# One hardware loop for the middle head groups, and the sum of |weight| gathered in one step instead of three

## The chip, the cores and the metric

The kernel runs on one core of a Trainium2 chip. The metric is the device time of one execution in microseconds (us); the kernel before took 2062.81 us, the median of three executions.

## The reference

Causal attention over 16 heads, then a feed-forward layer with ternary weights and 8-bit activations, and a residual:

```python
q, k, v = proj(x, Wq), proj(x, Wk), proj(x, Wv)      # x: 8 x 512 x 1024, fp32
scores = (q * beta) @ k.T / 8, causal; attn = softmax(scores)
a = (attn @ v) @ Wo.T
alpha = max(mean(|weight|), 1e-5)                     # one number
q_w = clip(round(weight / alpha), -1, 1) * alpha
q_a = round(a / s) * s,  s = max|a| over the row / 127
out = x + q_a @ q_w.T + bias
```

The scale alpha needs the sum of |weight| over the whole 1024 x 1024 matrix before the first weight can be rounded.

## The kernel before

The work is an order written out by hand, one list per engine. There are 4 groups `g` of 4 heads and 8 batches; a pair (group, batch) is an iteration `it`, 32 in all. Each iteration projects q, k and v for its batch (TensorE, `J(gi, k)`, line 170, in 8 accumulation groups `gi`), and has 16 units `u` = 4 heads x 4 query tiles. One unit is: scores `S(u)` (TensorE, lines 253 and 254), mask and row minimum `M(u)` (VectorE, 265), exponential `E(u)` (ScalarE, 272), reciprocal `I(u)` (VectorE, 278), normalisation (GpSimd, 284), transpose `T(u)` (TensorE, 294), its high part `H(u)` (ScalarE, 308) and low part `L(u)` (VectorE, 315). `PV(h)` (TensorE, 330) multiplies a head by v, `OL(h)` (ScalarE, 339) and `OA(h)` (VectorE, 347) add up its two halves. `V(gi)` takes a projection out of PSUM: the high part on ScalarE (201, 211, 217), the low part on VectorE (224, 231, 235). Every fp32 operand is split so into two parts.

A step overlaps the projections of iteration `now` with the later units of iteration `old` and the loading of x for `nxt`. `program` (line 682) calls the step function of each engine 33 times. The six inner batches of groups 0, 1 and 2 are hardware loops over `b`; the two steps between groups, which also split new weights (`qk_for`, `v_for`), and all steps of the last group are written out, so that their semaphore counts are constants.

The six inner steps of the last group carry `wf_part` = 0 to 5 and prepare the ternary weight. The weight comes as 8 tiles of 512 KB into two buffers (`load_wf`, line 448, on SP's DMA queue), once for the sum and once more for the rounding, 16 loads in all. A load waits until the tile two before it has been used. `wf_abs` (ScalarE, line 460) takes |tile| and its row sums:

```python
elif n < KT + 2:
    if due(count := n - 1):
        sp.wait_ge(wf_abs_done, count)
...
act.wait_ge(wf_in[k % 2], (k // 2 + 1) * 16)
act.activation(wf_raw[k % 2], wf_raw[k % 2], ACT.Abs, accum_out=wf_sums[:, k:k + 1])\
```

`wf_add_partitions` (TensorE) and `wf_scale` (VectorE) make alpha; `wf_ternary` (VectorE, three operations a tile) rounds. The sums of tiles 0 and 1 are taken late in the step of part 0, tiles 2 to 5 in part 1, tiles 6 and 7 early in part 2; alpha falls in part 2, and the rounding is in parts 2 to 5, two tiles each. SP issues the loads of the first two tiles right behind the four loads of x for the next iteration (`load_x`), and those of later tiles after the store of an output block (`store_o`) or around the two copies of k (`swap_k`).

After the last step, the output projection and the feed-forward layer run over 32 tiles of tokens.

Of the kernel before, what the change touches and what calls it, by code (L numbers as in the profile page):

```python
# [14 lines left out]
KT = D // P  # L15
HG = 4
NG = D // DH // HG
# [19 lines left out]
def adaln_ffn_kernel(nc, x, xT, cond, wq, wk, wv, wo, wf, bias, out):  # L37

    oT = nc.dram_tensor("oT_scratch", (KT, P, B, S), F32, kind="Internal").ap()
    with ExitStack() as ctx:  # L40
# [419 lines left out]
        def wf_abs(act, k):  # L460
            act.wait_ge(wf_in[k % 2], (k // 2 + 1) * 16)
            act.activation(wf_raw[k % 2], wf_raw[k % 2], ACT.Abs, accum_out=wf_sums[:, k:k + 1])\
               .then_inc(wf_abs_done, 1)
# [218 lines left out]
        def program(eng, step):  # L682
            step(eng, None, (0, 0, 0), (1, 1))
            with eng.Fori(1, B - 1) as b:
                step(eng, (b - 1, 0, b - 1), (b, 0, b), (b + 1, b + 1))
            for g in range(1, NG - 1):
                it = g * B
                step(eng, (it - 2, g - 1, B - 2), (it - 1, g - 1, B - 1), (it, 0), qk_for=g)
                step(eng, (it - 1, g - 1, B - 1), (it, g, 0), (it + 1, 1), v_for=g)
                with eng.Fori(1, B - 1) as b:  # L690
                    it = g * B + b
                    step(eng, (it - 1, g, b - 1), (it, g, b), (it + 1, b + 1))

            it, g = STEPS - B, NG - 1
            step(eng, (it - 2, g - 1, B - 2), (it - 1, g - 1, B - 1), (it, 0), qk_for=g)
            step(eng, (it - 1, g - 1, B - 1), (it, g, 0), (it + 1, 1), v_for=g)
            for b in range(1, B - 1):
                it = g * B + b
                step(eng, (it - 1, g, b - 1), (it, g, b), (it + 1, b + 1), wf_part=b - 1)
            it = STEPS - 1  # L700
            step(eng, (it - 1, g, B - 2), (it, g, B - 1), None, last=True)
            step(eng, (it, g, B - 1), None, None, last=True)

        def pe_step(pe, old, now, nxt, qk_for=None, v_for=None, wf_part=None, last=False):
            o, n, g = old and old[0], now and now[0], now and now[1]

            def J(gi, *ks):
                if now:
                    for k in ks:
                        project(pe, n, g, gi, k)  # L710

            def S(u):
                if u >= 8 and old:
                    scores(pe, o, u)
                elif u < 8 and now:
                    scores(pe, n, u)

            def T(u):
                if u >= 6 and old:
                    transpose(pe, o, u)  # L720
                elif u < 6 and now:
                    transpose(pe, n, u)

            def PV(h):
                if old:
                    times_v(pe, o, h)

            def Y(t, half, *ks):
                if last and not now:
                    for k in ks:  # L730
                        attention_out(pe, t, t, half, k)

            J(0, 0, 1, 2)
            S(8)
            T(6)
            J(0, 3, 4)
            PV(0)
            J(0, 5)
            S(9)
            T(7)  # L740
            J(0, 6, 7)
            J(1, 0)
            Y(0, 0, 0)
            S(10)
            T(8)
            J(1, 1, 2, 3)
            Y(0, 0, 1, 2, 3)
            S(11)
            T(9)
            J(1, 4)  # L750
            PV(1)
            J(1, 5, 6)
            Y(0, 0, 4, 5)
            S(12)
            T(10)
            J(1, 7)
            J(2, 0, 1)
            Y(0, 0, 6, 7)
            S(13)
            Y(0, 1, 0)  # L760
            T(11)
            J(2, 2, 3, 4)
            Y(0, 1, 1, 2)
            S(14)
            T(12)
            PV(2)
            J(2, 5, 6, 7)
            Y(0, 1, 3, 4)
            S(15)
            Y(0, 1, 5)  # L770
            T(13)
            J(3, 0, 1, 2)
            Y(0, 1, 6, 7)
            if wf_part == 2:
                wf_add_partitions(pe, n)
            S(0)
            T(14)
            J(3, 3, 4, 5)
            Y(1, 0, 0, 1)
            S(1)  # L780
            T(15)
            J(3, 6, 7)
            J(4, 0)
            Y(1, 0, 2, 3, 4, 5)
            S(2)
            T(0)
            PV(3)
            J(4, 1, 2, 3, 4, 5, 6)
            Y(1, 0, 6, 7)
            S(3)  # L790
            T(1)
            J(4, 7)
            J(5, 0, 1, 2, 3, 4)
            S(4)
            T(2)
            J(5, 5, 6, 7)
            J(6, 0, 1, 2)
            S(5)
            T(3)
            J(6, 3, 4, 5, 6, 7)  # L800
            J(7, 0)
            S(6)
            T(4)
            J(7, 1, 2, 3, 4, 5, 6)
            S(7)
            T(5)
            J(7, 7)

        def act_step(act, old, now, nxt, qk_for=None, v_for=None, wf_part=None, last=False):
# [3 lines left out]
            def E(u):  # L813
                if u >= 7 and old:
                    exponent(act, o, u)
                elif u < 7 and now:
                    exponent(act, n, u)

            def H(u):
                if u >= 5 and old:  # L820
                    pt_high(act, o, u)
                elif u < 5 and now:
                    pt_high(act, n, u)
# [15 lines left out]
                if qk_for is not None:  # L839
                    split_w_qk(act, n, qk_for, gi, False)  # L840

            def F(part, k):
                if wf_part == part:
                    wf_abs(act, k)

            if not old:
                split_w_qk(act, -1, 0, 0, False)
# [18 lines left out]
                split_w_v(act, o, v_for, False)  # L866
            H(6)
            E(8)
            F(1, 2)
            F(2, 6)  # L870
            OL(0)
            H(7)
            E(9)
            F(1, 3)
            F(2, 7)
            V(0)
            H(8)
            if ending:
# [2 lines left out]
            if ending:  # L881
                wo_high(act, 7)
                o_high(act, 1, 1)
            H(9)
            E(11)
            OL(1)
            H(10)
            E(12)
            V(1)
            H(11)  # L890
            E(13)
            H(12)
            E(14)
            F(0, 0)
            F(1, 4)
            OL(2)
            H(13)
            V(2)
            E(15)
            F(0, 1)  # L900
            F(1, 5)
            W(0)
            H(14)
            E(0)
# [32 lines left out]
        def dve_step(dve, old, now, nxt, qk_for=None, v_for=None, wf_part=None, last=False):  # L937
# [36 lines left out]
                    split_w_qk(dve, n, qk_for, gi, True)  # L974

            def Q(half):
                if wf_part is not None and 2 <= wf_part < 2 + KT // 2:
                    wf_ternary(dve, 2 * (wf_part - 2) + half)

            if not old:  # L980
                batch_scale(dve, 0, 0)
# [49 lines left out]
            L(13)  # L1031
            V(2)
            I(15)
            if wf_part == 2:
                wf_scale(dve, n)
            M(0)
            Q(0)
# [73 lines left out]
        def sp_step(sp, old, now, nxt, qk_for=None, v_for=None, wf_part=None, last=False):  # L1111
            ending = last and not now
            if not old:
                load_w(sp, 0, [0])
                load_x(sp, 0, 0)
                load_w(sp, 0, [1, 2])
            if qk_for is not None:
                load_w(sp, qk_for, [0, 1, 2])
            if nxt:
                load_x(sp, *nxt)  # L1120
            if wf_part == 0:
                load_wf(sp, 0)
                load_wf(sp, 1)
            if last and now:
                load_o(sp, 0, 0)
                load_o(sp, 1, 1)
            if ending:
                load_wo(sp, 6)
                load_wo(sp, 7)
            if old:  # L1130
                store_o(sp, *old, 0)
            if ending:
                load_o(sp, 2, 0)
            if wf_part == 1:
                load_wf(sp, 4)
                load_wf(sp, 5)
            if wf_part == 2:
                load_wf(sp, KT)
                load_wf(sp, KT + 1)
            if now:  # L1140
                swap_k(sp, now[0], 0)
            if last and now:
                load_wo(sp, 0)
                load_wo(sp, 1)
            if now:
                swap_k(sp, now[0], 1)
            if wf_part is not None and 2 <= wf_part < 1 + KT // 2:
                load_wf(sp, KT + 2 * wf_part - 2)
            if last and now:
                load_wo(sp, 2)  # L1150
            if old:
                store_o(sp, *old, 1)
            if wf_part is not None and wf_part < 2:
                load_wf(sp, 4 * wf_part + 2)
                load_wf(sp, 4 * wf_part + 3)
            if wf_part is not None and 2 <= wf_part < 1 + KT // 2:
                load_wf(sp, KT + 2 * wf_part - 1)
            if last and now:
                load_wo(sp, 3)
                load_wo(sp, 4)  # L1160
                load_wo(sp, 5)
# [133 lines left out]
```

## Time and profile before

| | us |
|---|---|
| median of three executions (2062.33 to 2063.89) | 2062.81 |
| the profiled execution's own time | 2063.89 |
| its span, first to last instruction | 2062.1 |
| TensorE busy, share of the span | 99% |
| VectorE, ScalarE, GpSimd busy | 62%, 49%, 39% |
| granted TensorE clock, mean | 0.999 |
| HBM read and written | 126.36 MB, 33.55 MB |

Times of the trace count from the start of the span. A busy share is an average: it tells what an engine did over the whole span, not whether it was waited for at a given place.

### The profile page before, as it was taken

Reading aid. Unit: us, or ns where it says so; the run is one execution under the profiler, and the core shown is the slowest. Engines: PE = TensorE matmul, PEld = TensorE weight load, DVE = VectorE, ACT = ScalarE, POOL = GpSimd, SP = SyncE. Lnnn points to the kernel's source line nnn. Section 1 sums busy time; section 2 is a strip of 40 time slices with the busy share of each in tenths; the row PEclk is TensorE's granted clock in tenths of the full one; section 3 lists DMA queues with packets and bytes.
Section 4 is the critical chain, followed back from the end, with each engine's and each line's share of the span. In section 5 each row is a group of like instructions: output and inputs, shape, how many; then the busy total and the mean of one; then the engine's idle time right before and its main releaser. Section 6 shows DMA issues by size and latency. Waiting matters only on the chain.

```text
span 2062.1 us, 36378 instructions
## 1 busy us (share of the span) xinstructions
PE 2035.6 (99%) x11747; PEld 1725.0 (84%) x11778; DVE 1274.7 (62%) x3163; ACT 1010.7 (49%) x2383; POOL 803.8 (39%) x746
## 2 busy tenths in 40 slices
PE   8999999999999999999999999999999999999998
PEld 7888888888888888888888888888887777777775
DVE  5666666766666667666666766667766545455454
ACT  5656556655656566666565766656565000000000
POOL 3433333433333334344433433333334544444441
PEclk9999999999999999999999999999999999999999
DMA  4222223222222242222224223323223432333322
GB/s 164 72 73 89 92 71 138 77 78 72 71 72 71 79 140 72 72 71 71 72 89 155 73 98 115 121 93 93 92 72 104 137 122 92 112 101 104 109 98 75
DMA packets 85936, 194.51 MB, mean 94 GB/s; under 512 B 7392, under 2 KB 40160, under 8 KB 84320
## 3 DMA queue, kind: packets, MB, share of 16 engines
q1 hardware_dynamic: 85856, 193.50, 29.3%
q8 instruction: 44, 0.72, 0.1%
q14 instruction: 36, 0.29, 0.0%
HBM read 126.36 MB, written 33.55 MB: 78 GB/s over the span
## 4 chain that ended last, share of the span: by engine, by line
PE 48%; issue 30%; POOL 19%; ACT 1%; DVE 1%; POOLq 1%; DMA 0%; DVEq 0%; SPq 0%; ACTq 0%
PE proj_ps L170 18%; POOL prob L284 12%; PE s_ps L563 9%; PE proj_ps L563 8%; POOL parts L374 7%; PE o_ps L634 5%; PE t_ps L294 3%; PE o_ps L330 2%; PE s_ps L254 1%; PE s_ps L253 1%; PE t_ps L612 1%; ACT parts L370 0%; POOLq L283 0%; DMA w_raw<-wq 0%; ACT v_st L201 0%
## 5 line engine op out<-in xcount | busy, mean ns | idle before, releaser
L170 PE MATMUL proj_ps<-parts 128*128 128x512 f32 (+1 forms) x6144 | 1214.3, 345 | 10.1 <-DVE parts L374 10.1
L170 PEld LDWEIGHTS proj_ps<-parts 128*128 128x128 f32 x6144 | 929.9, 190 | 119.5 <-issue 10.1
L284 POOL TENSOR_TENSOR prob<-prob,row_inv 128x128 f32<-128x128 f32 (+3 forms) x512 | 393.4, 771 | 932.3 <-DVE row_inv L278 929.9
L265 DVE CUSTOM_DVE_ANT_0 prob<-s_ps,mask 128x128 f32<-128x128 f32 (+3 forms) x512 | 249.8, 488 | 340.3 <-PE t_ps L294 194.3
L308 ACT ACTIVATE pt_hi<-t_ps 128x128 fp32r<-128x128 f32 (+3 forms) x512 | 222.3, 434 | 434.7 <-PE t_ps L294 430.4
L272 ACT ACTIVATE prob<-prob,row_min 128x128 f32<-128x128 f32 (+3 forms) x512 | 286.3, 559 | 72.9 <-DVE row_min L265 66.9
L315 DVE TENSOR_TENSOR pt_lo<-t_ps,pt_hi 128x128 fp32r<-128x128 f32 (+3 forms) x512 | 249.5, 487 | 65.5 <-ACT pt_hi L308 59.9
L619 ACT ACTIVATE yt_q<-t_ps 128x1024 bf16<-128x1024 bf16 x32 | 32.8, 1025 | 428.0 <-PE t_ps L612 428.0
L294 PE MATMUL t_ps<-ident,prob 128*128 128x128 f32 x1280 | 227.7, 276 | 7.3 <-POOL prob L284 5.7
L374 POOL TENSOR_TENSOR parts<-x_raw,parts 128x512 fp32r<-128x512 f32 x128 | 203.1, 1607 | 51.5 <-ACT parts L370 51.5
L563 PE MATMUL proj_ps<-parts 128*128 128x512 f32 x768 | 186.2, 396 | 0.0
L563 PE MATMUL s_ps<-parts 128*128 128x512 f32 x768 | 185.1, 396 | 0.0
L294 PEld LDWEIGHTS t_ps<-ident,prob 128*128 128x128 f32 x1280 | 150.8, 140 | 32.0 <-POOL prob L284 8.1
L563 PEld LDWEIGHTS s_ps<-parts 128*128 128x128 f32 x768 | 142.9, 188 | 30.6
L563 PEld LDWEIGHTS proj_ps<-parts 128*128 128x128 f32 x768 | 142.6, 188 | 30.3
L254 PE MATMUL s_ps<-k_st,q_st 128*128 128x128 f32 (+3 forms) x512 | 164.9, 322 | 0.0
L330 PE MATMUL o_ps<-pt_lo,v_st 128*128 128x512 f32 (+3 forms) x512 | 157.6, 319 | 0.5 <-DVE v_st L224 0.5
L253 PE MATMUL s_ps<-k_sw,q_st 128*128 128x128 f32 (+3 forms) x512 | 158.0, 309 | 0.0
L370 ACT ACTIVATE parts<-x_raw 128x512 fp32r<-128x512 f32 x256 | 147.0, 622 | 1.7 <-PE proj_ps L170 0.3
L330 PE MATMUL o_ps<-pt_hi,v_st 128*128 128x512 f32 (+3 forms) x512 | 146.5, 323 | 0.0
L374 DVE TENSOR_TENSOR parts<-x_raw,parts 128x512 fp32r<-128x512 f32 x128 | 135.8, 1080 | 8.1 <-ACT parts L370 8.0
L653 POOL TENSOR_TENSOR x_bias<-x_tile,bias_bc 128x1024 f32<-128x1024 f32 x32 | 76.2, 2384 | 105.2 <-DVE res L663 92.9
(65 smaller groups left out, 1902.9 us busy)
## 6 DMA issues: line engine op xcount, KB each, us to landing
x_raw<-xT SPq DMA_DIRECT2D x128, 512.0 KB, 5.5
k_sw<-k_st SPq DMA_DIRECT2D x128, 256.0 KB, 3.7
oT_scratch<-o_sum SPq DMA_DIRECT2D x64, 256.0 KB, 2.3
x_raw<-oT_scratch SPq DMA_DIRECT2D x32, 512.0 KB, 4.6
x_tile<-x SPq DMA_DIRECT2D x32, 512.0 KB, 5.2
out<-res SPq DMA_DIRECT2D x32, 512.0 KB, 3.1
w_raw<-wf SPq DMA_DIRECT2D x16, 512.0 KB, 5.6
w_raw<-wq SPq DMA_DIRECT2D x4, 1024.0 KB, 7.0
```

Of the source, the lines that this page charges most:

```text
L170: mm = pe.matmul(out, l, r, start=(k == 0 and i == 0), stop=(k == KT - 1 and i == 2))
L253: pe.matmul(s_ps[u % 2][:, 0:w], q, k_sw[:, h, 0:w], start=True, stop=False)
L254: pe.matmul(s_ps[u % 2][:, 0:w], q, k_st[:, h, 0:w], start=False, stop=True).then_inc(s_done, 1)
L265: dve.tensor_tensor_reduce(prob[:, u % 4, 0:w], s_ps[u % 2][:, 0:w], mask[:, S - w:S], 1.0, -MASKED, ALU.add, ALU.min, row_min[:, u % 4:u ...
L272: act.activation(prob[:, u % 4, 0:w], prob[:, u % 4, 0:w], ACT.Exp, bias=row_min[:, u % 4:u % 4 + 1], scale=-1.0, accum_out=row_sum[:, u % ...
L284: pool.tensor_tensor(prob[:, u % 4, 0:w], prob[:, u % 4, 0:w], row_inv[:, u % 4:u % 4 + 1].broadcast_to([P, w]), ALU.mult).then_inc(norm_d ...
L294: mm = pe.transpose(t_ps[u % 2][:, kb * P:(kb + 1) * P], prob[:, u % 4, kb * P:(kb + 1) * P], ident[:, :])
L308: act.activation(pt_view(pt_hi[h % 2], qt), t_ps[u % 2][:, 0:(qt + 1) * P] .rearrange("p (k q) -> p k q", q=P), ACT.Copy).then_inc(pt_hi_d ...
L315: dve.tensor_tensor(pt_view(pt_lo[h % 2], qt), t_ps[u % 2][:, 0:(qt + 1) * P] .rearrange("p (k q) -> p k q", q=P), pt_view(pt_hi[h % 2], q ...
L330: mm = pe.matmul(o_ps[h % 2][:, q0:S], v, part[h % 2][:, kb, q0:S], start=(kb == 0 and part is pt_lo), stop=(kb == QT - 1 and part is pt_hi))
L374: eng.tensor_tensor(x_lo[:, k, :], x_raw[:, k, :], x_hi[:, k, :].bitcast(F32), ALU.subtract).then_inc(x_lo_done[k % 2], 1)
L563: mm = pe.matmul(y_ps[p][half][:, :], a[p][:, o], b[k][:, w], start=(k == 0 and i == 0), stop=(k == KT - 1 and i == 2))
```

## The change

Two edits. The steps of groups 1 and 2 go into one hardware loop over `g` around the loop over `b`, so that the iteration number is made of two registers. And the eight sums of |tile| all go into the step of part 0, spread over ScalarE's list from behind `E(8)` on; alpha is made in part 1 and the rounding is in parts 1 to 4. SP's loads move with them.

```diff
-            for g in range(1, NG - 1):
+            with eng.Fori(1, NG - 1) as g:
                 it = g * B
...
-            if wf_part == 2:
+            if wf_part == 1:
                 wf_add_partitions(pe, n)
...
-            def F(part, k):
-                if wf_part == part:
-                    wf_abs(act, k)
+            def F(*ks):
+                if wf_part == 0:
+                    for k in ks:
+                        wf_abs(act, k)
...
             H(6)
             E(8)
-            F(1, 2)
-            F(2, 6)
+            F(0)
             OL(0)
             H(7)
             E(9)
-            F(1, 3)
-            F(2, 7)
+            F(1)
             V(0)
             H(8)
...
+            F(2)
             H(9)
             E(11)
+            F(3)
             OL(1)
             H(10)
+            F(4)
             E(12)
             V(1)
+            F(5)
             H(11)
             E(13)
+            F(6)
             H(12)
             E(14)
-            F(0, 0)
-            F(1, 4)
             OL(2)
+            F(7)
             H(13)
             V(2)
             E(15)
-            F(0, 1)
-            F(1, 5)
...
-                if wf_part is not None and 2 <= wf_part < 2 + KT // 2:
-                    wf_ternary(dve, 2 * (wf_part - 2) + half)
+                if wf_part is not None and 1 <= wf_part <= KT // 2:
+                    wf_ternary(dve, 2 * (wf_part - 1) + half)
...
             if nxt:
                 load_x(sp, *nxt)
             if wf_part == 0:
-                load_wf(sp, 0)
-                load_wf(sp, 1)
+                for i in range(6):
+                    load_wf(sp, i)
...
                 store_o(sp, *old, 0)
...
-            if wf_part == 1:
-                load_wf(sp, 4)
-                load_wf(sp, 5)
-            if wf_part == 2:
-                load_wf(sp, KT)
-                load_wf(sp, KT + 1)
+            if wf_part == 0:
+                load_wf(sp, 6)
             if now:
                 swap_k(sp, now[0], 0)
+            if wf_part == 0:
+                for i in range(7, KT + 2):
+                    load_wf(sp, i)
```

In parts 1 to 3 SP then loads the tiles 2 to 7 for the rounding at the same two places, before and after `store_o` of block 1, where parts 2 to 4 had them.

## Rows read from the trace of the kernel before

**Rows 1.** The page: busy time, share and instructions of each engine.

```profile
PE 2035.6 (99%) x11747; PEld 1725.0 (84%) x11778; DVE 1274.7 (62%) x3163; ACT 1010.7 (49%) x2383; POOL 803.8 (39%) x746
```

**Rows 2.** Timeline of PE, first product of `PV(0)` in six steps: start, duration, instruction.

```profile
443.73 0.39 PE L330 MATMUL o_ps<-pt_lo,v_st 128*128 128x512 f32 x1
...
687.33 0.39 PE L330 MATMUL o_ps<-pt_lo,v_st 128*128 128x512 f32 x1
...
736.06 0.39 PE L330 MATMUL o_ps<-pt_lo,v_st 128*128 128x512 f32 x1
...
1223.00 0.39 PE L330 MATMUL o_ps<-pt_lo,v_st 128*128 128x512 f32 x1
...
1320.29 0.39 PE L330 MATMUL o_ps<-pt_lo,v_st 128*128 128x512 f32 x1
...
1515.63 0.39 PE L330 MATMUL o_ps<-pt_lo,v_st 128*128 128x512 f32 x1
```

**Rows 3.** Timeline of SP in the step of part 0: start, time to issue.

```profile
1224.47 1.77 SPq L362 DMA_DIRECT2D x_raw<-xT  x4
1226.29 1.13 SPq L458 DMA_DIRECT2D w_raw<-wf  x2
...
1238.13 0.47 SPq L241 DMA_DIRECT2D k_sw<-k_st  x1
```

**Rows 4.** Issue to landing of single loads of wf, issued at 1226.29.

```profile
DMA to landing us min/median/max: 8.4/8.4/8.4
```

**Rows 5.** The same for loads issued at 1353.02, 1401.68 and 1407.67.

```profile
DMA to landing us min/median/max: 5.6/5.6/5.6
...
DMA to landing us min/median/max: 5.2/5.2/5.2
...
DMA to landing us min/median/max: 3.6/3.6/3.6
```

**Rows 6.** Timeline of ACT in the step of part 0, with idle time before.

```profile
1223.28 0.19 ACT L272 ACTIVATION_READ_ACCUMULATOR prob<-prob,row_min 128x1 f32 x1
...
1226.14 0.60 ACT L308 ACTIVATE pt_hi<-t_ps 128x512 fp32r<-128x512 f32 x1 [1.13 <-PE t_ps L294]
...
1227.54 1.40 ACT L211 ACTIVATE q_st<-proj_ps,q_scale 64x512 fp32r<-64x512 f32 x2 [0.31 <-PE proj_ps L170]
...
1232.13 0.72 ACT L272 ACTIVATE prob<-prob,row_min 128x512 f32<-128x512 f32 x1 [0.32 <-DVE row_min L265]
...
1236.09 1.20 ACT L217 ACTIVATE k_st<-proj_ps 64x512 fp32r<-64x512 f32 x2
...
1241.89 1.04 ACT L462 ACTIVATE w_raw<-w_raw 128x1024 f32<-128x1024 f32 x1
...
1243.05 0.60 ACT L339 ACTIVATE o_low<-o_ps 64x512 f32<-64x512 f32 x1
...
1244.93 1.38 ACT L211 ACTIVATE q_st<-proj_ps,q_scale 64x512 fp32r<-64x512 f32 x2
```

**Rows 7.** Timelines of POOL and DVE there: normalisation of units 9 and 15, `M(11)`.

```profile
1227.61 0.62 POOL L284 TENSOR_TENSOR prob<-prob,row_inv 128x256 f32<-128x256 f32 x1 [1.86 <-DVE row_inv L278]
...
1247.49 1.04 POOL L284 TENSOR_TENSOR prob<-prob,row_inv 128x512 f32<-128x512 f32 x1 [4.40 <-DVE row_inv L278]
...
1231.40 0.69 DVE L265 CUSTOM_DVE_ANT_0 prob<-s_ps,mask 128x512 f32<-128x512 f32 x1
```

**Rows 8.** Timeline of PE there: the transposes `T(9)` and `T(15)`.

```profile
1231.01 0.38 PE L294 MATMUL t_ps<-ident,prob 128*128 128x128 f32 x2
...
1249.36 0.60 PE L294 MATMUL t_ps<-ident,prob 128*128 128x128 f32 x4
```

**Rows 9.** Stretches: length, busy and count of each engine, granted clock, DMA share, GB/s.

```profile
10.10:14.80 4.70, 4.69 (x11) 3.69 (x12) 4.52 (x3) 3.12 (x7) 4.70 (x4) 1.00 1.03 432
20.00:24.70 4.70, 4.70 (x22) 3.68 (x21) 3.79 (x4) 1.83 (x3) 0.00 (x0) 1.00 0.70 279
...
2052.60:2056.00 3.40, 3.40 (x10) 1.23 (x9) 0.00 (x0) 0.00 (x0) 0.00 (x0) 0.50 0.38 154
```

More of the change, by code:

```diff
@@ L1033, in dve_step @@
             I(15)
-            if wf_part == 2:
+            if wf_part == 1:
                 wf_scale(dve, n)
@@ L1133, in sp_step @@
                 load_o(sp, 2, 0)
-            if wf_part == 1:
-                load_wf(sp, 4)
-                load_wf(sp, 5)
-            if wf_part == 2:
-                load_wf(sp, KT)
-                load_wf(sp, KT + 1)
+            if wf_part == 0:
+                load_wf(sp, 6)
             if now:
                 swap_k(sp, now[0], 0)
+            if wf_part == 0:
+                for i in range(7, KT + 2):
+                    load_wf(sp, i)
             if last and now:
@@ L1146, in sp_step @@
                 swap_k(sp, now[0], 1)
-            if wf_part is not None and 2 <= wf_part < 1 + KT // 2:
-                load_wf(sp, KT + 2 * wf_part - 2)
+            if wf_part is not None and 1 <= wf_part < KT // 2:
+                load_wf(sp, KT + 2 * wf_part)
             if last and now:
@@ L1152, in sp_step @@
                 store_o(sp, *old, 1)
[L1153 to L1157, printed above, removed]
+            if wf_part is not None and 1 <= wf_part < KT // 2:
+                load_wf(sp, KT + 2 * wf_part + 1)
             if last and now:
```

## The prediction

> **What bounds the kernel now.** I read the page first: TensorE is busy 99% of the span [rows 1]. So an edit can win little, and whatever makes TensorE wait is lost in full, since no later stage has idle time in which to make it good. Then I read the timeline of TensorE at the same mark of each step, the first product of `PV(0)`, to see what a step costs in its two forms [rows 2]. From 443.73 to 687.33 lie five steps of a hardware loop, each with a jump back: 48.72 us a step. From 687.33 to 736.06 lies the last one, which leaves the loop: 48.73. The two written-out steps from 1223.00 to 1320.29 (part 0 and part 1, with six of the eight sums) take 48.65 each, and the four from 1320.29 to 1515.63 (alpha and the rounding) 48.84 each. Last I read SP's, ScalarE's and the other engines' timelines within the step of part 0 and the landing of the loads, because the second edit puts all its work there.
>
> **The first edit, one loop over g.** Four steps that were written out (two between groups, for g = 1 and 2) get register counts. The loop form costs 48.72 - 48.65 = 0.07 us a step [rows 2], so 4 x 0.07 = 0.28 us. The twelve inner steps have one register more in their counts. No row shows such a step. Below, this costs nothing (counts may be kept in one register); above, as much again as the step from constants to one register did, 12 x 0.07 = 0.84. I take 0.2, nearer the lower end, since TensorE mostly has matmuls in its queue while its sequencer works; both ends stay for the range. The outer jump back is taken once. The inner jumps cost nothing that can be seen: 48.72 with them, 48.73 without [rows 2]. So I put it at nothing; its cover is the work already queued, and without that it would be well under a microsecond.
>
> [...]
>
> **The second edit, what only moves.** The eight sums are the same instructions. So are alpha and the 24 operations of the rounding; they come one step earlier, beside the same neighbours, and four steps keep their 48.84 - 48.65 = 0.19 us each. That is nothing net. The cover is the idle time of ScalarE and VectorE in steps that TensorE fills.
>
> **The second edit, the first tile.** Here lies the cost. Before, the first sum stands behind `E(14)`, at 1241.89 [rows 6]. Now `F(0)` stands right behind `E(8)`, whose last part starts at 1223.28 and ends at 1223.47 [rows 6]. But its tile is not there. SP issues the load behind the four loads of x, at 1226.29 [rows 3], and those four wait for the splits of x in this very step; neither is moved. The load takes 8.4 us to land, because 2 MB of x are ahead of it [rows 4]: 1234.7. ScalarE works in order. It stands at `F(0)` from 1223.5 to 1234.7, and behind it stand `OL(0)`, `H(7)`, `E(9)`, `V(0)` and all the rest; for `E(9)` waits `I(9)`, then the normalisation on GpSimd, then `T(9)`, and TensorE works in order too.
>
> The time at which `T(9)` can go follows in steps. A sum takes 1.16 us (1241.89 to the next start, 1243.05) [rows 6]: `F(0)` ends at 1235.85. `OL(0)` follows; the next can start about 0.5 us later: `H(7)` at 1236.35. From the start of `H(7)` at 1226.14 [rows 6] to the end of the normalisation of unit 9 at 1227.61 + 0.62 = 1228.23 [rows 7] lie 2.1 us. I add 0.25: on VectorE `OA(0)` now falls just ahead of `L(7)`, and the transpose starts a little after its release. So `T(9)` starts at 1238.7 instead of 1231.01 [rows 8]: **7.7 us**, all of it TensorE's. What stands before `T(9)` in its list does not hang on `F(0)`, so TensorE is idle for nearly all of that.
>
> **The second edit, the other tiles.** There are two buffers, so tile n + 2 is asked for only when sum n is done, and the whole chain is now in one step. A load with nothing ahead takes 3.6 us, one right behind the two copies of k takes 5.2 and 5.6 [rows 5]. Followed down ScalarE's list: `E(9)` ends 1.1 us after the start of `H(7)` (1227.54 less the idle 0.31, less 1226.14) [rows 6], at 1237.45. `F(1)` runs to 1238.6; its tile landed by then. `V(0)` starts there; `M(11)` on VectorE ended at 1231.40 + 0.69, 4.55 after the start of `V(0)` [rows 6, 7], so now at 1243.15. `E(11)` with its read-out takes 0.8: 1244.0. `F(3)` ends at 1245.15. (`F(2)` fits between, after `E(10)` at about 1241.3, and ends at 1242.45; tile 4 lands 3.7 later, 1246.15.) `OL(1)` and `H(10)` take 0.9, to 1246.05; `F(4)` ends at 1247.3, `E(12)` 0.4 later, `V(1)` takes 1.2 [rows 6] to 1248.95. Tile 5 landed at 1245.25 + 3.6 = 1248.85, so `F(5)` runs to 1250.1. SP is at the copies of k meanwhile: before they were issued at 1238.13 [rows 3], 2.04 after the start of `V(1)` at 1236.09 [rows 6]; now at 1247.75 + 2.04 = 1249.8, and they take 1.1 us to issue. Tile 7 is asked for at 1250.9, right behind them; with 5.4 (between the two rows) it lands at 1256.3. ScalarE reaches `F(7)` earlier, by about 1254.5, and waits. `F(7)` ends at 1257.5, `H(13)` 0.3 later, then comes `V(2)`. From the start of `V(2)` at 1244.93 [rows 6] to the end of the last normalisation at 1247.49 + 1.04 = 1248.53 [rows 7] lie 3.6 us. So `T(15)` can go at 1261.45 instead of 1249.36 [rows 8]: **12.1 us late**. This is a point in time set by ScalarE and SP, so it holds the first 7.7 in it and is not added. After `T(15)` ScalarE has no more sums, and its list has come level within a unit or two.
>
> Two things lie beneath that 12.1. The SP loads that now stand ahead of `store_o` wait for `F(3)` (1245.15), and the one ahead of the first copy of k for `F(4)` (1247.3). What they hold up is not due sooner: `store_o` needs `OA(1)`, some 1.2 us after `F(3)`, and the copies go at 1249.8. Loads 7 to 9 stand ahead of the second copies, but `F(7)` is done long before these are due.
>
> And the clock. The trace has TensorE at its lower level, 1.2 GHz, after idle time: a granted 0.50 in a stretch near the end, and at the start, after 10 us of nothing, 11 matmuls in 4.7 us where 22 of the same kind fit later (the granted clock is not recorded there, the rate shows it) [rows 9]. Seven idle microseconds will bring it down. At half rate for 3.4 to 4.7 us it loses 1.7 to 2.35 us. But TensorE would then reach `T(15)` 7.7 + 2.35 = 10.05 late at most, and is released at 12.1: the loss is hidden there. Only a second fall, after the 2 us of waiting at `T(15)`, would come on top, 1.7 us.
>
> **The sum.** 12.1 + 0.28 + 0.2 = 12.6 us. The profiled span of 2062.1 becomes 2074.7, and that execution's own 2063.9 becomes 2076.5. It was the slowest of three and lies 1.1 above their median, so the median goes from 2062.8 to **2075.4**, 0.6% slower.
>
> **The rivals.**
> *A, the first wait alone.* The later loads come fast enough, or the chain is shorter than I follow it, and `T(15)` is not late beyond what TensorE itself is. For it: tile 7 with 3.6 us instead of 5.4 makes `T(15)` 10.3 late, level with the first wait and its clock. Against: a load right behind the copies took 5.2 and 5.6 [rows 5]. Then 7.7 + 1.7 to 2.35 + 0.3 = 9.7 to 10.4: about 2073.
> *B, more than that.* The clock falls again at `T(15)` (1.7), or tile 6, the copies of k and tile 7 share the queue and each comes a microsecond later, and the loop costs its upper end. 12.1 + 1.7 + 1.1 + 1 = 15.9: up to 2078.7.
> *C, no loss that can be told.* The first tile is served beside the loads of x and not behind them. The load must land 0.7 us after its issue for no wait at all: the chain behind it must start 7.7 us sooner. At the shortest landing of any row, 3.6, it lands at 1229.9 and `T(9)` is 2.9 late; with the loop that is 2066. It decides below a landing of some 4.5 us. Against: 8.4 in this very place.
> *D, faster.* The nested loop would have to win something: the written-out steps would need a cost of their code that a loop saves. They are the shorter ones, by 0.07, so nothing speaks for it.
>
> **How the numbers follow.** My forecast has 0.6 (its own range 2073.8 to 2077), A 0.17, B 0.16, C 0.05, D 0.02. The range from 2071.5 to 2079.0 takes in A with the clock's lower loss and a little less, and all of B; some 1 in 10 is left outside. A measurement of this kernel can tell about 0.2%, 4.1 us, from no change. Slower by more than that: forecast, A, B, 0.93; within it 0.05; faster 0.02.
>
> **What will show it.** ScalarE's first sum waits for the DMA of wf for about 11 us from 1223.5. The step from `PV(0)` of part 0 to that of part 1 is about 12 us longer than 48.65, and no other step is longer by more than 0.2. `T(9)` waits over 7 us for GpSimd's normalisation, `T(15)` some 2. The granted clock falls to 0.50 once behind `T(9)`. The last sum waits for its load behind the copies of k. It is wrong if the first tile lands before 1230, if the steps in the nested loop grow by more than 0.1 each, or if TensorE makes up in later steps what it lost.

## The result and the profile after

The changed kernel takes 2079.3 us (median of four, 2075.96 to 2080.89) against 2062.8: ratio 1.0078, 95% interval 1.0059 to 1.0095, 16.5 us slower. The profiled execution has a span of 2076.9 us, 14.8 more than before.

The page, for the span and TensorE's busy time beside [rows 1]:

```profile
span 2076.9 us, 36984 instructions
...
PE 2040.9 (98%) x11778; PEld 1727.1 (83%) x11778; DVE 1276.6 (61%) x3163; ACT 1011.5 (49%) x2383; POOL 804.0 (39%) x746
```

The marks of the steps on TensorE's timeline, the first product of `PV(0)`, beside [rows 2]:

```profile
444.00 0.39 PE L330 MATMUL o_ps<-pt_lo,v_st 128*128 128x512 f32 x1
...
638.94 0.39 PE L330 MATMUL o_ps<-pt_lo,v_st 128*128 128x512 f32 x1
...
687.67 0.39 PE L330 MATMUL o_ps<-pt_lo,v_st 128*128 128x512 f32 x1
740.61 0.39 PE L330 MATMUL o_ps<-pt_lo,v_st 128*128 128x512 f32 x1
...
1227.33 0.39 PE L330 MATMUL o_ps<-pt_lo,v_st 128*128 128x512 f32 x1
1286.97 0.39 PE L330 MATMUL o_ps<-pt_lo,v_st 128*128 128x512 f32 x1
```

Two steps carry the loss. The step of part 0, from 1227.33 to 1286.97, is 59.64 us instead of 48.65: 11.0 more. And the step in which the loop over `g` jumps back, from 687.67 to 740.61, is 52.94 instead of 48.73: 4.2 more, of which the next step gives back 0.3. The inner steps of the nested loop (444.00 to 638.94, four of them) are still 48.73 each. 11.0 + 3.9 are 14.9, against 14.8 for the whole span.

ScalarE's timeline in the step of part 0: the first, sixth and seventh sum, each with its wait for the load, and the eighth, which has none, beside [rows 6].

```profile
1237.99 1.06 ACT L462 ACTIVATE w_raw<-w_raw 128x1024 f32<-128x1024 f32 x1 [10.20 <-DMA w_raw<-wf]
...
1252.70 1.06 ACT L462 ACTIVATE w_raw<-w_raw 128x1024 f32<-128x1024 f32 x1 [1.11 <-DMA w_raw<-wf]
...
1257.15 1.06 ACT L462 ACTIVATE w_raw<-w_raw 128x1024 f32<-128x1024 f32 x1 [2.19 <-DMA w_raw<-wf]
...
1259.58 1.05 ACT L462 ACTIVATE w_raw<-w_raw 128x1024 f32<-128x1024 f32 x1
```

TensorE's timeline, the instructions with idle time before them, around the jump (first line) and in the step of part 0: `T(9)`, `PV(2)`, `T(15)`, beside [rows 8].

```profile
734.96 3.90 PE L170 MATMUL proj_ps<-parts 128*128 128x512 f32 x9 [2.62 <-issue]
...
1241.92 0.69 PE L294 MATMUL t_ps<-ident,prob 128*128 128x128 f32 x2 [6.40 <-POOL prob L284]
...
1255.25 0.50 PE L330 MATMUL o_ps<-pt_lo,v_st 128*128 128x512 f32 x1 [1.42 <-DVE pt_lo L315]
...
1264.63 0.66 PE L294 MATMUL t_ps<-ident,prob 128*128 128x128 f32 x4 [0.16 <-POOL prob L284]
```

SP's timeline in that step, beside [rows 3], and under it the time to landing of three single loads of wf: tile 0 (issued 1230.62), tile 6 (1250.13) and tile 7 (1253.87), beside [rows 4, 5].

```profile
1228.81 1.77 SPq L362 DMA_DIRECT2D x_raw<-xT  x4
1230.62 17.01 SPq L458 DMA_DIRECT2D w_raw<-wf  x6
```

```profile
DMA to landing us min/median/max: 7.3/7.3/7.3
...
DMA to landing us min/median/max: 7.0/7.0/7.0
...
DMA to landing us min/median/max: 5.5/5.5/5.5
```

The stretches behind the jump and around `T(9)`, which starts at 1241.92: length, busy and count of each engine, granted clock (the last but two), beside [rows 9].

```profile
734.90:738.40 3.50, 3.44 (x8) 2.77 (x9) 0.69 (x1) 1.28 (x4) 1.34 (x2) 0.51 0.04 12
1240.20:1247.00 6.80, 5.08 (x16) 4.41 (x17) 4.60 (x13) 6.72 (x16) 1.93 (x3) 0.50 0.61 167
```

And the branch instruction on TensorE's sequencer (PEldq in the trace) at the end of a round of the loop over `g` (line 686), min/median/max in ns of the two:

```profile
L686 PEldq COMPARE_BRANCH  x2: 76/2232/4387, 730.2 to 1123.8; - x2
```

The jump that is not taken takes TensorE's sequencer 76 ns. The one that is taken holds it for 4387. TensorE runs out of matmuls in that time and is idle for 2.62 us, and its granted clock is 0.51 in the stretch of 3.50 us behind that.

### The profile page after: what moved, and what is told of

It is laid out like the page before. It is cut to its first block, busy times and chain, and to the rows that moved or that the text cites. A ratio compares the mean times of both kernels' runs of the same rounds, so it can differ in the third digit from the quotient of the medians.

```text
span 2076.9 us, 36984 instructions
## 1 busy us (share of the span) xinstructions
PE 2040.9 (98%) x11778; PEld 1727.1 (83%) x11778; DVE 1276.6 (61%) x3163; ACT 1011.5 (49%) x2383; POOL 804.0 (39%) x746
## 4 chain that ended last, share of the span: by engine, by line
PE 40%; issue 36%; POOL 20%; DMA 1%; ACT 1%; DVE 1%; POOLq 1%; SPq 0%; DVEq 0%; ACTq 0%
POOL prob L284 14%; PE proj_ps L170 12%; PE s_ps L563 8%; PE proj_ps L563 8%; POOL parts L374 6%; PE o_ps L634 5%; PE t_ps L294 2%; PE o_ps L330 2%; PE s_ps L254 1%; PE s_ps L253 1%; PE t_ps L612 1%; DMA w_raw<-wf 1%; POOLq L283 0%; DMA x_raw<-wo 0%; ACT parts L370 0%
## 5 line engine op out<-in xcount | busy, mean ns | idle before, releaser
L294 PEld LDWEIGHTS t_ps<-ident,prob 128*128 128x128 f32 x1280 | 150.8, 140 | 39.3 <-POOL prob L284 15.1
L347 DVE TENSOR_TENSOR o_sum<-o_ps,o_low 64x512 f32<-64x512 f32 x128 | 87.3, 682 | 52.1 <-ACT o_low L339 51.1
```

The source lines that it names most:

```text
L294: mm = pe.transpose(t_ps[u % 2][:, kb * P:(kb + 1) * P], prob[:, u % 4, kb * P:(kb + 1) * P], ident[:, :])
```

## The experiments

Times are medians of several executions, each against the kernel before on the same chip (2063.5 to 2063.9 us there). A step's length is read between marks as above, from one profiled execution of each kernel.

### The loop over g

**loop_only.** The first edit alone.

```diff
-            for g in range(1, NG - 1):
+            with eng.Fori(1, NG - 1) as g:
```

> The first edit alone: the loop over g, the sums of |weight| where they were. Theory (the jump back to a loop start that lies three step bodies behind makes the engine wait for its instructions): one step, the last of group 1, is 4.2 us longer than 48.7, TensorE's COMPARE_BRANCH there takes about 4.4 us, the granted clock falls to 0.50 for 3.4 us behind it; with 0.3 for four steps with register counts the kernel is 4.2 us slower, ratio 1.0020. Rival (the long step in the changed kernel came from something else, such as the register work of two nested loops or chance): no such step, and 0.3 to 1.1 us in all, ratio 1.0001 to 1.0005.

2067.15 us, +3.3: ratio 1.0015 (1.0006 to 1.0024). The sequencer's row and TensorE's timeline behind the jump:

```profile
L686 PEldq COMPARE_BRANCH  x2: 76/2222/4367, 729.9 to 1123.4; - x2
```

```profile
734.77 3.75 PE L170 MATMUL proj_ps<-parts 128*128 128x512 f32 x9 [2.68 <-issue]
```

The step is 52.81 long and no other is. So the long step is this edit's, and repeats: 4.1 over 48.71 in the profile, where the medians differ by 3.3.

The profile's DMA view also lists transfers of a kind that it calls instruction. From 729.9 to 734.5, the time of the branch, it has these (packets, MB, share):

```profile
q14 instruction: 3, 0.02, 2.3%
q8 instruction: 1, 0.02, 1.5%
```

In the kernel before, where the same steps are written out, it has none from 725 to 745.

**loop_pe and loop_not_pe.** The loop over `g` on TensorE alone, and on all engines but TensorE.

```diff
-            for g in range(1, NG - 1):
+            def middle(g):
...
+            if step is pe_step:            # loop_not_pe: is not
+                with eng.Fori(1, NG - 1) as g:
+                    middle(g)
+            else:
+                for g in range(1, NG - 1):
+                    middle(g)
```

> The loop over g on TensorE alone; the other four engines keep the written-out steps. Theory (TensorE's own wait for its instructions is the cost): the long step is there in full, 3.9 to 4.2 us, ratio 1.0020. Rival (ScalarE and VectorE, whose lists also stopped for about 3 us there, hold TensorE up): under 0.5 us.

> The loop over g on all engines but TensorE. In the changed kernel ScalarE took up its list late after the jump back, and its split of the last slice of x started at 737.50 instead of about 734.5. Theory: TensorE alone would reach T(7) 2.5 us after PV(0), at 738.9; GpSimd's split and normalisation behind ScalarE end at 740.5, so this costs 1.6 us, less than TensorE's own stop, ratio 1.0008 to 1.0010. Rival (the other engines carry the cost): 3.9 to 4.2 us.

loop_pe 2066.0 us, +2.1: 1.0010 (1.0001 to 1.0019). loop_not_pe 2067.26 us, +3.4: 1.0017 (1.0007 to 1.0026). In the profiles, the step with the jump is 52.78 and 51.24 us. TensorE's and ScalarE's timelines in loop_not_pe there:

```profile
738.68 0.47 PE L330 MATMUL o_ps<-pt_lo,v_st 128*128 128x512 f32 x1 [2.36 <-DVE pt_lo L315]
```

```profile
736.97 0.63 ACT L370 ACTIVATE parts<-x_raw 128x512 fp32r<-128x512 f32 x1 [1.70 <-issue]
```

TensorE does not stop itself here, but waits 2.36 us at `PV(0)` for a low part of VectorE (line 315). ScalarE stood for 1.70 us with nothing to wait for behind its own jump, and VectorE for 1.71 us ahead of its part of x at 735.79. I had put the cost of the other engines too low: 1.6 us, where that step is 2.5 longer and the median 3.4. The two stops lie beside each other and don't add: with both (loop_only) the step is 52.81, with TensorE's alone 52.78. Which costs more can't be told from the times. The profiles say TensorE's, the medians the other engines', and the intervals overlap. The instruction transfers tell the two apart: from 730 to 738 loop_pe has two, both on queue 8, and loop_not_pe one on queue 8 and six on queue 14.

**loop_hint.** The first edit alone, with a hint for the jump back of the loop over `g` (`hint_back_edge`).

```diff
+from concourse.ordered_engine_set import OrderedEngineSet
...
-            with eng.Fori(1, NG - 1) as g:
+            with nc.Fori(1, NG - 1, engines=OrderedEngineSet([eng.engine]), hint_back_edge=True) as g:
```

```profile
L687 PEldq COMPARE_BRANCH  x2: 85/224/363, 730.0 to 1119.7; - x2
```

The taken jump takes 363 ns instead of 4367. The registers, the nesting and the branch are all still there, and 2.7 of the 3.3 us are gone, so none of these was the cause. What TensorE waited for were in all likelihood the instructions at the jump's target: loop_only has two instruction transfers on queue 8 and five on queue 14 from 730 to 738. Here one is left from 730 to 740, on queue 8, and TensorE has no idle time from 728.73 to 737. How the hint brings this about, the traces do not show.

The interval of the 0.6 that is left takes in nothing at all. In the profiled execution most of it is not register counts. The four steps that got them are 0.07, 0.03, 0.11 and 0.01 us longer than before, 0.2 in all, and the inner steps have not grown. But the step from 1125.94, behind the loop over `g`, is 49.21 instead of 48.66: VectorE stands still in it for 1.72 us with nothing to wait for, and TensorE waits 0.28 for a low part behind that.

```profile
1141.09 0.17 DVE L279 RECIPROCAL row_inv<-row_sum 128x1 f32<-128x1 f32 x1 [1.72 <-issue]
```

**body2 and body3.** The kernel before, with two and with three steps in the body of each loop over the batches, nothing nested.

```diff
-                with eng.Fori(1, B - 1) as b:
-                    it = g * B + b
-                    step(...)
+                with eng.Fori(0, (B - 2) // m) as i:   # m = 2, 3
+                    for j in range(m):
+                        b = i * m + (1 + j)
+                        it = g * B + b
+                        step(...)
```

> The kernel before with two steps in the body of each hardware loop over the batches (three rounds instead of six; six jumps back in all instead of fifteen). TensorE's list is then about 1310 instructions a body, VectorE's 300, ScalarE's 255. [...] Two steps are not known: if TensorE's COMPARE_BRANCH stays at 0.2 us the time is that of the kernel before, within 0.5 us; if it takes over 4 us, each of six jumps costs 3 to 4 us, 18 to 24 in all. [...]

> The same with three steps in the body, two rounds, three jumps back in all, none nested: as long as the body of the loop over g, about 1960 instructions on TensorE. Theory (length of the body): every one of the three jumps holds TensorE's sequencer about 4.4 us and costs 3 to 4 us, 9 to 12 us in all, ratio 1.0045 to 1.006. Rival (the nesting of the two loops was the cause): like the kernel before, within 0.5 us.

body2 2070.27 us, +6.8: 1.0035 (1.0023 to 1.0047). body3 2068.79 us, +5.3: 1.0024 (1.0015 to 1.0034). The sequencer's rows of line 692 (groups 1 and 2), body3 and then body2:

```profile
L692 PEldq COMPARE_BRANCH  x4: 76/1883/3707, 584.8 to 1123.0; - x4
```

```profile
L692 PEldq COMPARE_BRANCH  x6: 76/212/217, 534.6 to 1124.3; - x6
```

With three steps TensorE's sequencer stops 3.6 to 3.7 us at each of the three jumps, without any nesting, so the nesting is not the cause. The size was missed: the granted clock stayed at 1.00 in the 3.5 us behind each of the three waits (from 197.4, 588.8 and 979.6), and a jump cost 1.7 us and less, where I expected 3 to 4. The line of TensorE's timeline behind the one at 584.79:

```profile
588.86 2.35 PE L170 MATMUL proj_ps<-parts 128*128 128x512 f32 x9 [1.68 <-DVE parts L374]
```

The profile puts this wait down to VectorE, whose part of x was done at 588.55. TensorE's sequencer came back from its branch at 588.48, so either would have held TensorE until then; this run does not part the two.

With two steps TensorE does not stop (217 ns), and I expected the time of the kernel before, within 0.5 us. It is 6.8 slower. The cause is VectorE. TensorE's and VectorE's timelines behind the first jump of group 1 in body2:

```profile
543.45 0.50 PE L330 MATMUL o_ps<-pt_lo,v_st 128*128 128x512 f32 x1 [2.26 <-DVE v_st L224]
```

```profile
542.79 0.42 DVE L224 TENSOR_TENSOR v_st<-proj_ps,v_st 128x256 fp32r<-128x256 f32 x1 [1.51 <-issue]
```

VectorE waits here for nothing that the profile shows, and it is its second stop behind this jump: another of 1.46 us ends at 540.40. Its body of two steps is 292 instructions, TensorE's 1304, by the records between two marks. The two jumps of group 1 make a step 51.0 to 51.1 us long; those of group 2, with one stop of 1.4 us and one of 0.7 each, 49.5; and those of group 0, with a body of the same length and no stop, 48.7. The instruction transfers go with the stops. From 534 to 546, around the first jump of group 1, there are three on queue 14:

```profile
q14 instruction: 3, 0.02, 0.9%
```

On that queue there are also three around each of the other jumps of groups 1 and 2, and no instruction transfer at all from 144 to 155 and from 241 to 255, around those of group 0. So what VectorE waits for are in all likelihood its instructions, and the length of the body alone does not decide whether it has to. What else does is not shown.

### The eight sums

**sums_only.** The second edit alone; the steps between the groups are written out as before.

> The second edit alone: written-out steps, all eight sums in part 0. Theory: the step of part 0 is 59.6 us instead of 48.65, as in the changed kernel, and no other step moves; 11 us in the profiled execution, ratio 1.0050 to 1.0065. Rival (part of the long step in the changed kernel came from the loop edit, by way of the code that is fetched): 9 us or less.

2075.16 us, +11.7: 1.0054 (1.0037 to 1.0071). The step of part 0 is 60.5 us, 0.9 more than I expected. TensorE's waits in it, and the stretch from 1251.70 with its granted clock:

```profile
1238.01 0.69 PE L294 MATMUL t_ps<-ident,prob 128*128 128x128 f32 x2 [6.40 <-POOL prob L284]
...
1251.03 0.50 PE L330 MATMUL o_ps<-pt_lo,v_st 128*128 128x512 f32 x1 [1.84 <-DVE pt_lo L315]
```

```profile
1251.70:1255.10 3.40, 3.40 (x12) 2.94 (x11) 1.14 (x3) 1.63 (x6) 0.86 (x2) 0.50 0.84 283
```

The granted clock fell to 0.50 a second time here, behind `PV(2)`, where the changed kernel has 1.00 (from 1255.20 to 1258.70).

Both edits alone add up to 15.0 us, within the interval of the 16.5 of the two together.

**sums_early.** As sums_only, but tiles 0 and 1 are loaded ahead of x.

```diff
+            if wf_part == 0:
+                load_wf(sp, 0)
+                load_wf(sp, 1)
             if nxt:
                 load_x(sp, *nxt)
             if wf_part == 0:
-                for i in range(6):
+                for i in range(2, 6):
                     load_wf(sp, i)
```

> The second edit alone, with the loads of tiles 0 and 1 issued ahead of the four loads of x, so that the first two sums find their tiles there. Theory (two separate costs, the first wait of 6.6 us with its clock loss, and behind it the chain sum, load, sum through two buffers): the first wait goes, tile 2 now lands at about 1234.5 behind x, and the chain still makes PV(2) and T(15) late; the step is 4 to 6 us longer than 48.65. Rival (the first wait is the whole cost): under 0.5 us. Second rival (the cost is ScalarE's 9 us of work in one step, wherever the tiles are): as long as before, 9 to 11 us.

2070.22 us, +6.7: 1.0031 (1.0020 to 1.0043). The step is 55.1 us, 6.5 longer than 48.65, just above the 4 to 6 expected. ScalarE's third sum, and TensorE at `PV(2)`:

```profile
1233.80 1.06 ACT L462 ACTIVATE w_raw<-w_raw 128x1024 f32<-128x1024 f32 x1 [2.99 <-DMA w_raw<-wf]
```

```profile
1244.71 0.80 PE L330 MATMUL o_ps<-pt_lo,v_st 128*128 128x512 f32 x1 [3.40 <-DVE pt_lo L315]
```

`T(9)` no longer waits. The wait has moved down the list: tile 2 is now the one behind x, and the chain through two buffers ends at `PV(2)`. So the early place of the first sum is not the whole cost; five microseconds of it were had back by the order of the loads, and the rest was not.

**sums_no_reload.** As sums_only, but only tiles 0 and 1 are loaded, and each is summed four times. It leaves out the sums of tiles 2 to 7.

```diff
-            act.wait_ge(wf_in[k % 2], (k // 2 + 1) * 16)
+            act.wait_ge(wf_in[k % 2], 16)
+            if k >= 2:
+                act.wait_ge(wf_abs_done, k - 1)
...
-                for i in range(6):
+                for i in range(2):
                     load_wf(sp, i)
...
-            if wf_part == 0:
-                load_wf(sp, 6)
...
-                for i in range(7, KT + 2):
+                for i in range(KT, KT + 2):
                     load_wf(sp, i)
```

> The second edit alone, with tiles 0 and 1 loaded where they were, and each of them summed four times, so that no sum waits for a reload. It leaves out the sums of tiles 2 to 7. Theory: T(9) is 6.6 us late as before, the clock loses 2.3, and what came behind it (1.7 at PV(2), 0.3 at T(15)) goes: 8.9 to 9.3 us. Rival (the chain of loads adds nothing, ScalarE's work does): 11 us as with all tiles.

2072.81 us, +9.3: 1.0045 (1.0028 to 1.0061). The step is 57.65 us, 9.0 over 48.65. TensorE's waits:

```profile
1237.58 0.69 PE L294 MATMUL t_ps<-ident,prob 128*128 128x128 f32 x2 [6.27 <-POOL prob L284]
...
1249.41 0.50 PE L330 MATMUL o_ps<-pt_lo,v_st 128*128 128x512 f32 x1 [0.35 <-DVE pt_lo L315]
```

The first wait stays, that at `PV(2)` goes from 1.84 to 0.35. Behind the first wait, the chain of reloads costs the difference of the two steps, 60.5 - 57.65 = 2.9 us.

**sums_no_dma.** Both: tiles 0 and 1 ahead of x, each summed four times. It leaves out the same sums.

> Both together: tiles 0 and 1 loaded ahead of x, each summed four times, at the eight places of the change. It leaves out the sums of tiles 2 to 7. Theory (only waits for DMA cost, ScalarE has room for eight sums of 1.16 us in one step): the step of part 0 is 48.6 to 48.9 us, the kernel like the one before, ratio 0.9995 to 1.0005. Rival (the work itself makes later units late): 1 to 3 us.

2064.75 us, +1.3: 1.0006 (0.9996 to 1.0016). The step is 49.28 us. TensorE's one wait that is new:

```profile
1241.35 0.50 PE L330 MATMUL o_ps<-pt_lo,v_st 128*128 128x512 f32 x1 [0.34 <-DVE pt_lo L315]
```

Eight sums of ScalarE's time in one step cost 0.6 us, a little more than I expected (0 to 0.25). The rest, 60.5 - 49.3 = 11.2 us, is waiting for DMA and what follows from it. Its two parts are not independent: the first wait costs 57.65 - 49.28 = 8.4 us by itself and the chain 2.9 on top of it, but without the first wait (sums_early) the chain costs 55.12 - 49.28 = 5.8.

### A version that beats both

**swap7 and swap7_flat.** In the kernel before, `T(7)` waits for GpSimd in each step. swap7 is that kernel with GpSimd's normalisation of unit 7 moved ahead of its split of the last slice of x; swap7_flat has all steps written out as well.

```diff
-            elif now:
-                x_low(pool, n, 7)
...
             for u in range(7, UNITS):
                 if old:
                     normalise(pool, o, u)
+                    if u == 7 and now:
+                        x_low(pool, n, 7)
```

> A version for its own sake: the kernel before, with GpSimd's normalisation of unit 7 ahead of its split of the last slice of x. In the kernel before T(7) waits 0.2 to 0.3 us for this normalisation in every step, at 2.45 to 2.53 us after PV(0), and is the only wait of TensorE in a step. If that is so, each of 31 steps is 0.2 to 0.3 us shorter, 6 to 9 us in all, ratio 0.9955 to 0.997. Against it: the split of the slice is 1 us later, and if the product that needs it waits instead, nothing is won.

> The same, and all steps written out, without hardware loops over the batches: the opposite of the first edit. The 18 loop steps were 0.07 us longer than the written-out ones; as that difference lay at T(7)'s wait, most of it should be gone with the reordering already: 0 to 1.3 us less than with the reordering alone. Rival (the longer code has to be fetched and costs that): 1 us or more above it.

swap7 2054.0 us: ratio 0.9952 (0.9938 to 0.9967), 9.5 us faster, a little more than the 6 to 9 expected. swap7_flat 2053.36 us: 0.9950 (0.9936 to 0.9964). GpSimd's and TensorE's timelines in one step of swap7, after `PV(0)` at 537.84:

```profile
537.95 1.04 POOL L284 TENSOR_TENSOR prob<-prob,row_inv 128x512 f32<-128x512 f32 x1
538.95 1.29 POOL L374 TENSOR_TENSOR parts<-x_raw,parts 128x512 fp32r<-128x512 f32 x1
```

```profile
540.05 0.60 PE L294 MATMUL t_ps<-ident,prob 128*128 128x128 f32 x4
```

The normalisation ends 1 us before `T(7)`, which now starts 2.21 us after `PV(0)` with no idle time before it. Every step up to part 1, in a loop or written out, is 48.36 to 48.37 us: 0.36 less in a loop, 0.3 less written out. So the 0.07 us between the two forms lay at that one wait and is gone with it. That it was register work of TensorE's sequencer is argued, not shown.

## Why the prediction was right, and where it was not

**The first tile: right, 1.1 us too much.** The place, the mechanism and the order are as followed. The load took 7.3 us, not 8.4, and so `T(9)` came 6.6 us late (14.59 us after `PV(0)`, before 8.01 [rows 2, 8]) instead of 7.7. Nearly all of the 1.1 is in that landing.

**The chain to `T(15)`: right in kind, nearly right in size, and in part by luck.** `T(15)` came 37.30 us after `PV(0)` instead of 26.36 [rows 2, 8]: 10.9 late, where I had 12.1. That it is ScalarE and its loads which set this time is right; the loads are not the ones I followed. I had the last sum wait for tile 7, and none of tiles 1 to 6 hold ScalarE up by more than a little. Tile 7 was asked for 26.5 us after `PV(0)`, 1.4 sooner than I had it, and took 5.5 us, where I had 5.4. It landed at 1259.35, and the last sum, at 1259.58, did not wait for it. ScalarE came there only then because tile 6 had taken 7.0 us: the seventh sum had waited 2.19 for it, and the sixth 1.11 for tile 5. Rival B had tile 6 and tile 7 late beside the copies of k; tile 6 was. The two ways to the last sum end within 0.2 us of each other here, and so the error in tile 6 does not show in the sum. What I did not see either is where TensorE would stand meanwhile. I had it waiting 2 us at `T(15)`; it waited 1.42 at `PV(2)`, for a low part behind the sixth sum, and only 0.16 at `T(15)`. The sum did not change by that, since ScalarE sets the end.

**The clock: right in kind, low for longer.** The traces give it only as a granted share. What stands beside the 1.2 GHz of my forecast is the rate: 11 products of 512 columns in 4.7 us [rows 9] are 1.2 columns a ns. The granted clock was 0.50 for 6.8 us, from ahead of `T(9)` on, and TensorE was busy for 5.1 of them, where I had 3.4 to 4.7. `T(12)` was 8.9 us late against the 6.6 of `T(9)`, so it cost 2.3, and the waits at `PV(2)` and `T(15)` would have been longer without it. As forecast, it was hidden. The second fall that I feared is not there in this execution, but sums_only has one behind `PV(2)`.

**Register counts: small, as said, and smaller.** In the profile of the hinted loop the four steps that got them grew by 0.2 us together, where I had 0.28, and the twelve inner steps did not grow (48.73 in the changed kernel), where I had 0.2. The medians can't tell so little from nothing.

**The outer jump: wrong.** This is the term that was mis-sized. I put it at nothing because the inner jumps "cost nothing that can be seen", and its worst case at "well under a microsecond". No row stood behind that worst case. The trace before has this for the jumps over one step in groups 1 and 2:

```profile
L690 PEldq COMPARE_BRANCH  x12: 76/208/223, 486.0 to 1119.2; - x12
```

The outer jump costs 3.9 us in the profile. By the medians the whole loop edit costs 3.3, of which 2.7 go with the hint. With 3.9 for it the sum is 10.9 + 0.3 + 3.9 = 15.1 for the profiled execution, against 14.8. Mostly because of this term the median, 2079.3, is 3.9 above my forecast of 2075.4. That is outside the forecast's own range (2073.8 to 2077) and 0.3 above the upper end of the whole range, 2079.0, which the interval of the ratio takes in on both sides (2062.8 x 1.0059 to 1.0095 is 2075.0 to 2082.4). The range came as close as it did because of rival B, whose own grounds for a time so late (the clock falling again, the loop's register counts at their upper end) did not come true. The argument was from a jump over one step's instructions to a jump over three steps'. The row I used, 48.72 with and 48.73 without a jump, is true of a body of some 650 instructions on TensorE and says nothing of one three times as long.

What the runs show of the stop is this. A taken jump over one or two steps held TensorE's sequencer 0.2 us, over three steps 3.6 to 4.4 us with instruction transfers in that time, and 0.36 us with the hint. The bodies of two steps in body2 are 1304 instructions by the records, those of three in body3 are 1955. At which length in between the stop begins, and whether the length is all that counts, is not shown.

**The moved rounding: right.** The four steps with alpha and the rounding took 48.93, 48.83, 48.83 and 48.83 us, now from part 1 on.

## What to carry to other kernels

Before a piece of work is moved forward in an engine's list, read when its DMA can land at the new place, and what stands ahead of it in the DMA queue: here eight sums of 1.2 us had room in one step (they cost 0.6 us), and the first wait, for one 512 KB load behind 2 MB, cost 8.4 us, seven times the work of the sum that waited. Judge a loop's jump back by the number of instructions it goes back over on each engine, not by shorter jumps in the same kernel (TensorE's sequencer was held 0.2 us over 1304 instructions and 3.7 over 1955), and look in the profile of the result, since VectorE's jumps over equally long bodies differed; the hint for the jump brought TensorE's 4.4 us down to 0.36. And look at the one short wait that every step has: some 0.3 us at the same instruction in 31 steps were worth 9.5 us.

## What was not expected of the hardware

A taken jump held TensorE's sequencer 4.4 us (three steps back, nested), 3.6 to 3.7 us (three steps, not nested), 0.36 us with a hint, and 0.2 us over one or two steps. VectorE stopped behind a jump over 292 instructions twice for about 1.5 us in one group, for 1.4 and 0.7 us in another, and in the third, with a body of the same length, not at all; what differs is left open. TensorE, idle for only 2.6 to 2.7 us, had a granted clock of 0.51 in the next 3.4 to 3.5 us in the changed kernel, in loop_only and in loop_pe, while behind waits of 2.26 us in body2 and 2.36 in loop_not_pe it had 1.00 over 3.5 us. In sums_only a wait of 1.84 us was followed by 3.4 us at 0.50; there the granted clock had been 0.50 until 1241.5, ten microseconds earlier. So the length of the wait alone does not tell.
